# Attention on one core: rings of three PSUM banks for score tiles and row halves, and five instead of six key steps summed on GpSimd

## The chip, the cores and the metric

One core of a Trainium2 chip runs the kernel. The metric is the device time of one execution in microseconds, the median of several.

## The reference, cut to what matters

The input is 8 samples of 256 channels on 32 x 32 positions. Four residual blocks follow one another: a state-space block, an attention block, a block of dilated convolutions, and a second attention block with layer norms around it. All of it is fp32. Both attentions have 8 heads of width 32 over 1024 positions:

```python
x = x + _L0_conv_ref(_gn(x), ...)
x = x + _L1_conv_ref(_gn(x), ...)      # attention
x = x + _L2_conv_ref(_gn(x), ...)
x = x + _L3_conv_ref(_gn(x), ...)      # layer norm, attention, layer norm
# within an attention
scores = jnp.einsum('bthe,bThe->bhtT', q, k) / jnp.sqrt(jnp.float32(EMB))
attn = jax.nn.softmax(scores, axis=-1)
out = jnp.einsum('bhtT,bThe->bthe', attn, v)
```

## The kernel before

The samples run one after the other, and each has two attentions, so there are 16 in all. The five engines have each a program of their own, written out by hand, and wait for each other by counters (`Signal`). The order of each engine's work is the order of its loops.

An attention has four phases (`PHASES`): two groups of four heads (`GH`), times two halves of 512 queries (`NC`). The softmax needs the largest score of each query first, and for that the scores are computed twice:

- **Row halves.** `row_scores(n, cc)` (L1239) computes a 128 x 512 piece of the scores with queries on the partitions, and VectorE reduces it to a maximum per query (`row_max`, L954). A phase needs 32 of them. Those of phase 0 run ahead of the phases. Those of phase ph + 1 are laid between the work of phase ph, `HALF_ROWS` = 5, 4, 4, 4, 5, 5, 5, 0 for its key steps 0 to 7. The last phase has none to do.
- **The turn.** When the 32 are done, VectorE joins them (`mboth`), TensorE transposes them (`turn_max`), ScalarE and VectorE make the negated maxima (`nm`) and SyncE copies these into `QS` by DMA, where they take part in the next phase's score matmuls.
- **Tiles.** A phase has 8 key steps (`KT`). For each, TensorE computes four score tiles of 128 keys x 512 queries, one per head (L1340), and ScalarE takes the exponential from PSUM to the buffer `PT` (L624), which has room for three key steps.
- **Values.** `values(i - 1)` (L1281) multiplies the weights of the key step before with V, four matmuls in four column groups (L1292, eight passes in the trace), which add up in bank 0.
- **Denominators.** The weights must be summed over the keys. Most key steps of a phase are added up element by element on GpSimd (L408, `POOL_SUMS`), in the last phase on VectorE (L1006, `DVE_SUMS`), into `acc`, and one group of matmuls sums `acc` over the partitions into bank 1 (L1311). The key steps that are in no such list are summed on TensorE directly, by four more matmuls with ones (L1301) behind their values.

PSUM has eight banks. In the phases bank 0 holds the output, bank 1 the denominators, banks 2 to 5 the four tiles of a key step, and banks 6 and 7 the two halves of one row. An exponential covers two tiles (1024 columns), and a pair of tiles waits until the exponential of the same pair of the key step before is done. A row half waits for the maximum of the row before (L1249). TensorE's order in key step kt is: tile, tile, row half, tile, tile, row half, values of step kt - 1, then what is left of the row halves, one of them between the values and the direct sum where there is one.

Of the kernel before, what the change touches and what calls it, by code (L numbers as in the profile page):

```python
# [23 lines left out]
P = 128  # L24
# [4 lines left out]
NC = L // N  # L29
HEADS, DH = 8, 32  # L30
GH = 4
GROUPS = HEADS // GH
KT = L // P
# [19 lines left out]
TURN_AT = 7  # L53
AHEAD = 3
NORM_AT = 4
PHASE_ROWS = sum(HALF_ROWS) // NC

POOL_SUMS = (0, 1, 2, 3, 5, 6)
DVE_SUMS = (0, 1, 2, 3, 4, 5, 6)
SMALL_U = 1.0 / 128  # L60

# [31 lines left out]
def build(nc, x, wpack, vpack, w8, out):  # L93
    with ExitStack() as ctx:
        sb = lambda name, shape, dt=F32: ctx.enter_context(nc.sbuf_tensor(name, shape, dt))

        def sig(name, per):
            return Signal(ctx.enter_context(nc.semaphore(name)), per)
# [145 lines left out]
        nm_in = sig("nm_in", 2 * PHASES * 2 * 16)  # L244
        sum_pool = sig("sum_pool", 2 * (PHASES - 1) * (len(POOL_SUMS) - 1))
        sum_dve = sig("sum_dve", 2 * (len(DVE_SUMS) - 1))
        s_ps, p_sb = sig("s_ps", 128), sig("p_sb", 128)
        pv_ps, den_ln, den_rc = sig("pv_ps", 64), sig("den_ln", 8), sig("den_rc", 8)
        o_raw, o_sb = sig("o_raw", 8), sig("o_sb", 8)

# [80 lines left out]
        def _(pool):  # L331
# [35 lines left out]
            def sample(b):  # L367
# [27 lines left out]
                for a in range(2):  # L395
                    for j in range(GH):
                        pool.wait_ge(*stackedq[1][j](b, (a + 1) * 48))
                        pool.wait_ge(*stackedk[1][j](b, (a + 1) * 48))
                    for ph in range(PHASES - 1):
                        if ph == 2:  # L400
                            pool.wait_ge(*pv_ps(b, (PHASES * a + 1) * KT))
                        for k in range(1, len(POOL_SUMS)):
                            i, total = key_step(a, ph, POOL_SUMS[k]), acc[:, ph % 2, :, :]
                            first = PT[:, key_step(a, ph, 0) % 3, :, :] if k == 1 else total
                            if k > 1:
                                pool.wait_ge(*sum_pool(b, pool_sums(a, ph, k - 1)))
                            pool.wait_ge(*p_sb(b, 2 * i + 2))
                            pool.tensor_tensor(total, first, PT[:, i % 3, :, :], ALU.add).then_inc(sum_pool.sem, 1)  # L408
                pool.wait_ge(*x_new(b, 16))

# [5 lines left out]
        def _(act):  # L416
# [160 lines left out]
            def attention(b, a):  # L577
# [34 lines left out]
                for ph in range(PHASES):  # L612
                    for kt in range(KT):
                        i = key_step(a, ph, kt)
                        if kt == 0 and ph >= 1:
                            reciprocals(PHASES * a + ph - 1)
                        if i % (PHASES * KT) >= 3:
                            act.wait_ge(*pv_ps(b, i - 2))
                            done = summed(a, *divmod(i % (PHASES * KT) - 3, KT))
                            if done:  # L620
                                act.wait_ge(*(sum_pool, sum_dve)[done[0]](b, done[1]))
                        for pr in range(2):
                            act.wait_ge(*s_ps(b, 2 * i + pr + 1))
                            act.activation(PT[:, i % 3, 2 * pr:2 * pr + 2, :], PS[:, 2 + 2 * pr:4 + 2 * pr, :],  # L624
                                           ACT.Exp, scale=SCALE).then_inc(p_sb.sem, 1)
                        if kt == TURN_AT and ph < PHASES - 1:
                            neg_max(ph + 1)
# [41 lines left out]
        def _(dve):  # L669
# [269 lines left out]
            def attention(b, a):  # L939
# [60 lines left out]
                for k in range(1, len(DVE_SUMS)):  # L1000
                    i, total = key_step(a, ph, DVE_SUMS[k]), acc[:, ph % 2, :, :]
                    first = PT[:, key_step(a, ph, 0) % 3, :, :] if k == 1 else total
                    if k > 1:
                        dve.wait_ge(*sum_dve(b, dve_sums(a, k - 1)))
                    dve.wait_ge(*p_sb(b, 2 * i + 2))
                    dve.tensor_tensor(total, first, PT[:, i % 3, :, :], ALU.add).then_inc(sum_dve.sem, 1)  # L1006
                normalize(ph)

# [54 lines left out]
        def _(pe):  # L1063
# [161 lines left out]
            def attention(b, a, X):  # L1225
# [13 lines left out]
                def row_scores(n, cc):  # L1239
# [4 lines left out]
                    if c == 0 and q == 0 and cc == 0:  # L1244
                        pe.wait_ge(*stackedq[g][j](b, (a + 1) * 48))
                        pe.wait_ge(*stackedk[g][j](b, (a + 1) * 48))
                    ahead = 2 if ph == 0 else 1
                    if n % PHASE_ROWS >= ahead:
                        pe.wait_ge(*r_max(b, halves(a, n - ahead, cc) + 1))  # L1249
                    pe.matmul(PS[:, row_slot(n, cc), :], QS[0:kd, c, h, q * P:q * P + P], KS[0:kd, h, cc * N:cc * N + N],  # L1250
                              start=True, stop=True).then_inc(r_ps.sem, 1)

# [28 lines left out]
                def values(i, between, turn=None):  # L1281
# [2 lines left out]
                    g = ph // NC  # L1284
                    sums = POOL_SUMS if ph < PHASES - 1 else DVE_SUMS
                    direct = [k for k in range(KT) if k not in sums]
                    pe.wait_ge(*p_sb(b, 2 * i + 2))
                    if kt == 0 and ph > 0:
                        pe.wait_ge(*o_raw(b, i // KT))
                    for j in range(GH):  # L1290
# [24 lines left out]
                for ph in range(PHASES):  # L1315
# [10 lines left out]
                    for kt in range(KT):  # L1326
                        i = key_step(a, ph, kt)
                        row[1] = HALF_ROWS[kt]
                        if kt == 0:
# [2 lines left out]
                            else:  # L1332
                                next_rows(NC)
                            pe.wait_ge(*nm_in(b, 32 * (PHASES * a + ph + 1)))
                        for pr in range(2):
                            if ph + kt > 0:
                                pe.wait_ge(*p_sb(b, 2 * i - 2 + pr + 1))
                            for jj in range(2):
                                h = GH * g + 2 * pr + jj
                                ins = pe.matmul(PS[:, 2 + 2 * pr + jj, :], KS[:, h, kt * P:kt * P + P], QS[:, c, h, :],  # L1340
                                                start=True, stop=True)
                            ins.then_inc(s_ps.sem, 1)
                            next_rows(1)
                        if kt > 0:
                            values(i - 1, next_rows, ph + 1 if kt == TURN_AT and ph < PHASES - 1 else None)
                        next_rows(row[1])
                values(key_step(a, PHASES - 1, KT - 1), lambda most: None)

# [57 lines left out]

def row_slot(n, cc):

    return (4 + 2 * (n % 2) if n < PHASE_ROWS else 6) + cc


def halves(a, n, cc):
# [112 lines left out]
```

## Time and profile before

| | |
|---|---|
| median of 3 runs | 5492.75 us (5491.58 to 5498.53) |
| the profiled execution | 5495.14 us, its span 5493.3 us |
| granted TensorE clock over the span | 0.853 of full speed |
| TensorE matmul busy | 4249.1 us (77%) |
| VectorE busy | 3607.0 us (66%) |
| ScalarE busy | 2146.6 us (39%) |
| GpSimd busy | 2007.6 us (37%) |
| chain that ended last, by engine | TensorE 47%, VectorE 28%, issue 10%, ScalarE 7% |

Busy time says how long an engine was at work, and not whether somebody waited for it. The chain is followed back from the last instruction to what released it, and its shares say on whose work the end depended. In the timeline equal neighbouring instructions are drawn together (x8 is eight of them), the brackets give how long the engine was idle before them and whose work came last, and PEld is the load of the weights for a matmul.

### The profile page before, as it was taken

The numbers are of one execution on the slowest core, as the hardware profiler recorded it, in microseconds if no ns is written. First come the engines' busy times: TensorE is split into PE (matmuls) and PEld (weight loads), VectorE is DVE, ScalarE is ACT, GpSimd is POOL, SyncE is SP. The second block draws the span as 40 slices with busy tenths as digits, with TensorE's granted clock in tenths as the row PEclk, the third lists the DMA queues.
The fourth block names the chain that finished last, engine by engine and source line by source line (L and its number), as shares of the span: only waits on it lengthen the run. The fifth ranks groups of instructions, "written<-read, shape, count | busy, mean of one in ns | idle before, by whom it ended". The sixth has DMA issues, their size and how long they took to land.

```text
span 5493.3 us, 44457 instructions
## 1 busy us (share of the span) xinstructions
PE 4249.1 (77%) x16298; PEld 1843.1 (34%) x16298; DVE 3607.0 (66%) x4793; ACT 2146.6 (39%) x2639; POOL 2007.6 (37%) x681
## 2 busy tenths in 40 slices
PE   5688866879668896688866878669796697866978
PEld 2243422434224332243322433224332243322333
DVE  6763677637776368764687646867468674686746
ACT  3233452334423354243542425424254242542524
POOL 3531435404344043440444504434044340443404
PEclk7689977999769997799977999779897798977999
DMA  0020100210002100022000120011200112001020
GB/s 36 0 55 19 29 8 7 48 29 19 8 8 47 34 14 8 9 47 44 3 8 14 41 46 1 8 25 30 46 1 8 31 24 46 1 8 29 19 46 9
DMA packets 62956, 125.75 MB, mean 23 GB/s; under 512 B 18825, under 2 KB 21001, under 8 KB 62482
## 3 DMA queue, kind: packets, MB, share of 16 engines
q1 hardware_dynamic: 62738, 122.91, 9.6%
q8 instruction: 129, 2.11, 0.2%
q14 instruction: 89, 0.73, 0.0%
HBM read 12.23 MB, written 8.39 MB: 4 GB/s over the span
## 4 chain that ended last, share of the span: by engine, by line
PE 47%; DVE 28%; issue 10%; ACT 7%; SPq 4%; POOL 2%; DMA 2%; DVEq 0%; ACTq 0%; POOLq 0%
DVE mx L954 9%; PE PS L1250 8%; PE PS L1292 8%; PE PS L1087 7%; PE PS L1340 7%; PE PS L1374 4%; DVE work L846 3%; DVE work L848 3%; PE PS L1146 3%; PE PS L1184 2%; ACT PT L624 2%; SPq L290 2%; PE PS L1301 2%; SPq L299 2%; POOL work L392 1%
## 5 line engine op out<-in xcount | busy, mean ns | idle before, releaser
L954 DVE TENSOR_REDUCE mx<-PS 128x1 f32<-128x512 f32 x2048 | 1338.1, 687 | 422.0 <-PE PS L1250 417.9
L624 ACT ACTIVATE PT<-PS 128x1024 f32<-128x1024 f32 x1024 | 1006.9, 1023 | 689.9 <-PE PS L1340 660.0
L1250 PE MATMUL PS<-KS,QS 96*128 96x512 f32 x2048 | 894.9, 479 | 195.4 <-DMA KS<-piece 84.7
L408 POOL TENSOR_TENSOR piece<-PT 128x2048 f32<-128x2048 f32 x48 | 220.0, 4584 | 2183.4 <-ACT PT L624 2183.4
L408 POOL TENSOR_TENSOR piece<-piece,PT 128x2048 f32<-128x2048 f32 x192 | 878.0, 4573 | 58.4 <-ACT PT L624 47.1
L388 POOL TENSOR_TENSOR work<-work,Crep 128x1024 f32<-128x1024 f32 x256 | 616.3, 2409 | 390.5 <-DVE work L846 193.1
L1340 PE MATMUL PS<-QS,KS 98*128 98x512 f32 x2048 | 681.4, 424 | 45.9 <-DMA QS<-nm 22.2
L1250 PEld LDWEIGHTS PS<-KS,QS 96*128 96x128 f32 x2048 | 378.0, 197 | 816.2 <-DVE mx L954 578.0
L1292 PE MATMUL PS<-PT,Vt 128*32 128x512 f32 x4096 | 546.0, 605 | 27.0 <-ACT PT L624 27.0
L1184 PE MATMUL PS<-dstk,sel 128*128 128x512 f32 (+1 forms) x640 | 315.7, 568 | 321.1 <-DVE work L848 133.0
L542 ACT ACTIVATE PS<-PS,Aneg 128x1024 f32<-128x1024 f32 x256 | 278.3, 1087 | 628.5 <-PE PS L1184 597.8
L1184 PE MATMUL PS<-ustk,sel 128*128 128x512 f32 (+1 forms) x640 | 335.3, 597 | 182.9 <-DVE work L831 85.6
L1340 PEld LDWEIGHTS PS<-QS,KS 98*128 98x128 f32 x2048 | 376.5, 197 | 291.0 <-ACT PT L624 164.5
L1087 PE MATMUL PS<-xg,W 128*128 128x512 f32 x640 | 354.0, 709 | 81.1 <-ACT Brep L470 36.3
L1184 PEld LDWEIGHTS PS<-dstk,sel 128*128 128x128 f32 x640 | 152.9, 268 | 460.5 <-DVE work L846 178.9
L1184 PEld LDWEIGHTS PS<-ustk,sel 128*128 128x128 f32 x640 | 139.7, 257 | 491.1 <-DVE work L831 170.5
L1146 PE MATMUL PS<-work,ysel 128*32 128x512 f32 (+1 forms) x1536 | 273.1, 802 | 39.3 <-POOL work L392 30.6
L831 DVE TENSOR_TENSOR work<-PS,Brep 128x1024 f32<-128x1024 f32 (+1 forms) x256 | 250.7, 979 | 71.7 <-PE PS L1184 68.8
L946 DVE SCALAR_TENSOR_TENSOR piece<-PS,V,piece 128x1024 fp32r<-128x1024 f32 x64 | 82.2, 1284 | 278.1 <-ACT piece L588 278.1
L392 POOL TENSOR_TENSOR work<-work,Crep 128x640 f32<-128x640 f32 x128 | 210.5, 1648 | 138.7 <-DVE work L857 80.4
L373 POOL TENSOR_TENSOR ustk<-work,ustk 64x1024 fp32r<-64x1024 f32 x16 | 37.6, 2352 | 587.9 <-ACT ustk L485 587.3
L1087 PEld LDWEIGHTS PS<-xg,W 128*128 128x128 f32 x640 | 144.7, 231 | 263.2 <-issue 182.6
(198 smaller groups left out, 4983.0 us busy)
## 6 DMA issues: line engine op xcount, KB each, us to landing
QS<-piece SPq DMA_DIRECT2D x384, 128.0 KB, 2.4
KS<-piece SPq DMA_DIRECT2D x384, 128.0 KB, 2.4
xin<-x SPq DMA_DIRECT2D x8, 1024.0 KB
out<-xr SPq DMA_DIRECT2D x8, 1024.0 KB, 4.0
W<-wpack SPq DMA_DIRECT2D x2, 1024.0 KB
QS<-nm SPq DMA_DIRECT2D x128, 8.0 KB, 1.9
W<-wpack SPq DMA_DIRECT2D x1, 576.0 KB
W<-wpack SPq DMA_DIRECT2D x2, 256.0 KB
```

Of the source, the lines that this page charges most:

```text
L388: pool.tensor_tensor(slot, h, Crep[:, at:at + L], ALU.mult).then_inc(hC_sb.sem, 1)
L392: pool.tensor_tensor(two(slot), two(h), Crep[:, None, at:at + W3].broadcast_to((P, 2, W3)), ALU.mult).then_inc(hC_sb.sem, 1)
L408: pool.tensor_tensor(total, first, PT[:, i % 3, :, :], ALU.add).then_inc(sum_pool.sem, 1)
L542: act.activation(dst, src, ACT.Exp, scale=Aneg[:, ps * SG + g:ps * SG + g + 1]).then_inc(dA_sb.sem, 1)
L624: act.activation(PT[:, i % 3, 2 * pr:2 * pr + 2, :], PS[:, 2 + 2 * pr:4 + 2 * pr, :], ACT.Exp, scale=SCALE).then_inc(p_sb.sem, 1)
L954: dve.tensor_reduce(mx[:, at, cc:cc + 1], PS[:, row_slot(n, cc), :], AX.X, ALU.max).then_inc(r_max.sem, 1)
L1087: ins = pe.matmul(PS[:, bank, :], w[:, k, m * P:m * P + P], X[:, k, c * N:c * N + N], start=(k == 0), stop=(k == CT - 1))
L1146: ins = pe.matmul(PS[32 * j:32 * j + 32, c, 0:N if ps < 2 else W3], ysel[:, q % 4, :], src, start=(q % 4 == 0), stop=(q % 4 == 3), skip_gr ...
L1184: ins = pe.matmul(PS[:, slot + c, 0:wc], sel[:, g % 8, :], stk[:, g // 8, at + c * N:at + c * N + wc], start=True, stop=True)
L1250: pe.matmul(PS[:, row_slot(n, cc), :], QS[0:kd, c, h, q * P:q * P + P], KS[0:kd, h, cc * N:cc * N + N], start=True, stop=True).then_inc(r_ ...
L1292: ins = pe.matmul(PS[32 * j:32 * j + 32, 0, :], Vt[:, kt, DH * h:DH * h + DH], PT[:, i % 3, j, :], start=(kt == 0), stop=(kt == KT - 1), s ...
L1340: ins = pe.matmul(PS[:, 2 + 2 * pr + jj, :], KS[:, h, kt * P:kt * P + P], QS[:, c, h, :], start=True, stop=True)
```

## The change

- Constants: a ring size of three, and `POOL_SUMS` is (0, 1, 3, 4, 6) instead of (0, 1, 2, 3, 5, 6). Key steps 2, 5 and 7 of phases 0 to 2 are then summed directly on TensorE, where it was 4 and 7.
- Tiles take banks 2, 3 and 4 in turn, each tile by itself: it waits for the exponential three tiles back, and has a signal of its own. The exponential covers one tile (512 columns), four per key step where there were two.
- Row halves of phases 1 to 3 take banks 5, 6 and 7 in turn and wait for the maximum three halves back. Phase 0 stays at banks 4 to 7 and the wait of four halves.
- TensorE's order in key step kt is: tile, row half, tile, row half, values of step kt - 1 (with a row half ahead of the direct sum, where there is one), tile, row half, tile, row half.
- Who waits for the weights of a key step counts four signals instead of two.

```diff
--- before.py
+++ after.py
@@ -53,9 +53,10 @@
 TURN_AT = 7
 AHEAD = 3
 NORM_AT = 4
+RING = 3
 PHASE_ROWS = sum(HALF_ROWS) // NC
 
-POOL_SUMS = (0, 1, 2, 3, 5, 6)
+POOL_SUMS = (0, 1, 3, 4, 6)
 DVE_SUMS = (0, 1, 2, 3, 4, 5, 6)
 SMALL_U = 1.0 / 128
 
@@ -244,7 +245,7 @@
         nm_in = sig("nm_in", 2 * PHASES * 2 * 16)
         sum_pool = sig("sum_pool", 2 * (PHASES - 1) * (len(POOL_SUMS) - 1))
         sum_dve = sig("sum_dve", 2 * (len(DVE_SUMS) - 1))
-        s_ps, p_sb = sig("s_ps", 128), sig("p_sb", 128)
+        s_ps, p_sb = sig("s_ps", 256), sig("p_sb", 256)
         pv_ps, den_ln, den_rc = sig("pv_ps", 64), sig("den_ln", 8), sig("den_rc", 8)
         o_raw, o_sb = sig("o_raw", 8), sig("o_sb", 8)
 
@@ -404,7 +405,7 @@
                             first = PT[:, key_step(a, ph, 0) % 3, :, :] if k == 1 else total
                             if k > 1:
                                 pool.wait_ge(*sum_pool(b, pool_sums(a, ph, k - 1)))
-                            pool.wait_ge(*p_sb(b, 2 * i + 2))
+                            pool.wait_ge(*p_sb(b, GH * i + GH))
                             pool.tensor_tensor(total, first, PT[:, i % 3, :, :], ALU.add).then_inc(sum_pool.sem, 1)
                 pool.wait_ge(*x_new(b, 16))
 
@@ -619,9 +620,9 @@
                             done = summed(a, *divmod(i % (PHASES * KT) - 3, KT))
                             if done:
                                 act.wait_ge(*(sum_pool, sum_dve)[done[0]](b, done[1]))
-                        for pr in range(2):
-                            act.wait_ge(*s_ps(b, 2 * i + pr + 1))
-                            act.activation(PT[:, i % 3, 2 * pr:2 * pr + 2, :], PS[:, 2 + 2 * pr:4 + 2 * pr, :],
+                        for j in range(GH):
+                            act.wait_ge(*s_ps(b, GH * i + j + 1))
+                            act.activation(PT[:, i % 3, j, :], PS[:, score_slot(i % (PHASES * KT), j), :],
                                            ACT.Exp, scale=SCALE).then_inc(p_sb.sem, 1)
                         if kt == TURN_AT and ph < PHASES - 1:
                             neg_max(ph + 1)
@@ -1002,7 +1003,7 @@
                     first = PT[:, key_step(a, ph, 0) % 3, :, :] if k == 1 else total
                     if k > 1:
                         dve.wait_ge(*sum_dve(b, dve_sums(a, k - 1)))
-                    dve.wait_ge(*p_sb(b, 2 * i + 2))
+                    dve.wait_ge(*p_sb(b, GH * i + GH))
                     dve.tensor_tensor(total, first, PT[:, i % 3, :, :], ALU.add).then_inc(sum_dve.sem, 1)
                 normalize(ph)
 
@@ -1244,9 +1245,9 @@
                     if c == 0 and q == 0 and cc == 0:
                         pe.wait_ge(*stackedq[g][j](b, (a + 1) * 48))
                         pe.wait_ge(*stackedk[g][j](b, (a + 1) * 48))
-                    ahead = 2 if ph == 0 else 1
-                    if n % PHASE_ROWS >= ahead:
-                        pe.wait_ge(*r_max(b, halves(a, n - ahead, cc) + 1))
+                    ahead = 2 * NC if ph == 0 else RING
+                    if NC * (n % PHASE_ROWS) + cc >= ahead:
+                        pe.wait_ge(*r_max(b, halves(a, n, cc) - ahead + 1))
                     pe.matmul(PS[:, row_slot(n, cc), :], QS[0:kd, c, h, q * P:q * P + P], KS[0:kd, h, cc * N:cc * N + N],
                               start=True, stop=True).then_inc(r_ps.sem, 1)
 
@@ -1284,7 +1285,7 @@
                     g = ph // NC
                     sums = POOL_SUMS if ph < PHASES - 1 else DVE_SUMS
                     direct = [k for k in range(KT) if k not in sums]
-                    pe.wait_ge(*p_sb(b, 2 * i + 2))
+                    pe.wait_ge(*p_sb(b, GH * i + GH))
                     if kt == 0 and ph > 0:
                         pe.wait_ge(*o_raw(b, i // KT))
                     for j in range(GH):
@@ -1332,17 +1333,14 @@
                             else:
                                 next_rows(NC)
                             pe.wait_ge(*nm_in(b, 32 * (PHASES * a + ph + 1)))
-                        for pr in range(2):
-                            if ph + kt > 0:
-                                pe.wait_ge(*p_sb(b, 2 * i - 2 + pr + 1))
-                            for jj in range(2):
-                                h = GH * g + 2 * pr + jj
-                                ins = pe.matmul(PS[:, 2 + 2 * pr + jj, :], KS[:, h, kt * P:kt * P + P], QS[:, c, h, :],
-                                                start=True, stop=True)
-                            ins.then_inc(s_ps.sem, 1)
+                        for j in range(GH):
+                            if GH * (KT * ph + kt) + j >= RING:
+                                pe.wait_ge(*p_sb(b, GH * i + j - RING + 1))
+                            pe.matmul(PS[:, score_slot(i % (PHASES * KT), j), :], KS[:, GH * g + j, kt * P:kt * P + P],
+                                      QS[:, c, GH * g + j, :], start=True, stop=True).then_inc(s_ps.sem, 1)
                             next_rows(1)
-                        if kt > 0:
-                            values(i - 1, next_rows, ph + 1 if kt == TURN_AT and ph < PHASES - 1 else None)
+                            if j == 1 and kt > 0:
+                                values(i - 1, lambda most: next_rows(1) if most == 1 else None, ph + 1 if kt == TURN_AT and ph < PHASES - 1 else None)
                         next_rows(row[1])
                 values(key_step(a, PHASES - 1, KT - 1), lambda most: None)
 
@@ -1406,7 +1404,12 @@
 
 def row_slot(n, cc):
 
-    return (4 + 2 * (n % 2) if n < PHASE_ROWS else 6) + cc
+    return 4 + 2 * (n % 2) + cc if n < PHASE_ROWS else 5 + (NC * (n % PHASE_ROWS) + cc) % RING
+
+
+def score_slot(i, j):
+
+    return 2 + (GH * i + j) % RING
 
 
 def halves(a, n, cc):
```

## Rows read from the trace of the kernel before

**Rows 1.** Costliest groups (page, section 5): busy us, mean ns, idle before, releaser

```profile
L954 DVE TENSOR_REDUCE mx<-PS 128x1 f32<-128x512 f32 x2048 | 1338.1, 687 | 422.0 <-PE PS L1250 417.9
L624 ACT ACTIVATE PT<-PS 128x1024 f32<-128x1024 f32 x1024 | 1006.9, 1023 | 689.9 <-PE PS L1340 660.0
...
L408 POOL TENSOR_TENSOR piece<-piece,PT 128x2048 f32<-128x2048 f32 x192 | 878.0, 4573 | 58.4 <-ACT PT L624 47.1
```

**Rows 2.** Busy time by stretch: phases 0, 1 and 3 of the first attention

```profile
328.28:361.29 33.01, 29.55 (x133) 14.29 (x137) 21.81 (x34) 16.14 (x17) 22.60 (x5) 0.88 0.01 1
361.29:394.27 32.98, 30.77 (x157) 12.70 (x159) 22.92 (x36) 17.01 (x19) 22.91 (x6) 1.00 0.01 2
...
427.24:454.16 26.92, 22.61 (x136) 7.25 (x135) 16.39 (x11) 17.85 (x20) 0.25 (x1) 1.00 0.01 1
```

**Rows 3.** Timeline, an ordinary key step: start us, length us, engine line operation [idle before]

```profile
340.09 1.06 PE L1292 MATMUL PS<-PT,Vt 128*32 128x512 f32 x8
341.08 0.30 PEld L1250 LDWEIGHTS PS<-KS,QS 96*128 96x128 f32 x2 [0.84 <-DVE mx L954]
...
341.62 2.68 DVE L954 TENSOR_REDUCE mx<-PS 128x1 f32<-128x512 f32 x4 [0.73 <-PE PS L1250]
341.65 0.62 PE L1340 MATMUL PS<-QS,KS 98*128 98x512 f32 x2
342.36 0.19 PEld L1250 LDWEIGHTS PS<-KS,QS 96*128 96x128 f32 x1 [0.52 <-DVE mx L954]
...
342.70 0.63 PE L1340 MATMUL PS<-QS,KS 98*128 98x512 f32 x2
...
343.17 0.40 PE L1250 MATMUL PS<-KS,QS 96*128 96x512 f32 x1
...
343.50 1.06 PE L1292 MATMUL PS<-PT,Vt 128*32 128x512 f32 x8
```

**Rows 4.** Timeline, a key step whose weights TensorE sums directly

```profile
351.00 1.07 PE L1292 MATMUL PS<-PT,Vt 128*32 128x512 f32 x8
...
352.42 1.07 PE L1301 MATMUL PS<-PT,ones 128*32 128x512 f32 x8
...
353.42 0.30 PEld L1250 LDWEIGHTS PS<-KS,QS 96*128 96x128 f32 x2 [0.84 <-DVE mx L954]
```

**Rows 5.** Timeline, from one phase to the next

```profile
359.19 1.94 ACT L624 ACTIVATE PT<-PS 128x1024 f32<-128x1024 f32 x2 [2.45 <-PE PS L1340]
...
359.48 1.06 PE L1292 MATMUL PS<-PT,Vt 128*32 128x512 f32 x8
...
361.18 1.07 PE L1292 MATMUL PS<-PT,Vt 128*32 128x512 f32 x8 [0.43 <-ACT PT L624]
...
364.03 1.06 PE L1311 MATMUL PS<-piece,ones 128*32 128x512 f32 x8
...
366.33 3.85 ACT L624 ACTIVATE PT<-PS 128x1024 f32<-128x1024 f32 x4
...
369.62 1.07 PE L1292 MATMUL PS<-PT,Vt 128*32 128x512 f32 x8
```

**Rows 6.** Timeline, the last phase

```profile
427.12 1.07 PE L1292 MATMUL PS<-PT,Vt 128*32 128x512 f32 x8 [0.42 <-ACT PT L624]
...
430.00 0.77 PEld L1340 LDWEIGHTS PS<-QS,KS 98*128 98x128 f32 x4 [1.01 <-DMA QS<-nm]
...
433.78 1.07 PE L1292 MATMUL PS<-PT,Vt 128*32 128x512 f32 x8
...
438.26 1.06 PE L1292 MATMUL PS<-PT,Vt 128*32 128x512 f32 x8
...
440.11 1.94 ACT L624 ACTIVATE PT<-PS 128x1024 f32<-128x1024 f32 x2 [0.42 <-PE PS L1340]
...
448.75 1.07 PE L1292 MATMUL PS<-PT,Vt 128*32 128x512 f32 x8 [0.42 <-ACT PT L624]
```

**Rows 7.** Groups by line and shape, ScalarE on one bank

```profile
L605 ACT ACTIVATE lr<-PS 128x512 f32<-128x512 f32 x64 | 38.2, 597 | 215.3 <-PE PS L1311 215.3
```

## The prediction

> **What bounds the kernel now.** I read three views: the costliest groups, then the busy time of each engine phase by phase, then the timeline of single key steps. In the groups [rows 1] the reader is to see that VectorE's row maxima and ScalarE's exponentials spend a third to two thirds of a busy time waiting for TensorE, so neither sets the pace, and that one GpSimd sum takes 4.57 us. By stretch [rows 2] a phase with row halves lasts 33.0 us, of which TensorE is busy 30.8, VectorE 22.9, GpSimd 22.9 and ScalarE 17.0. The last phase has no row halves and lasts 26.9 us. TensorE is thus the nearest bound, and the question is what its order waits for.
>
> I call V(k) the values group of key step k (eight passes), T0 to T3 the four score tiles of a step, R a row half, D the four direct sums of the weights. In an ordinary step [rows 3] one V starts at 340.09 and the next at 343.50, so 3.41 us. Inside it: V holds TensorE for 0.99 us before the next weight load, and its next matmul starts about 1.10 us after V did. Two matmuls take 0.47 us (342.70 to 343.17), so 0.235 each; a matmul ahead of a V takes 0.33. One R waits for VectorE's maximum (load at 342.36, where without the wait it would be at 342.0). With four R, four T and a V and no wait the step is 7 x 0.235 + 0.33 + 1.10 = 3.08 us. So 0.33 us of a step is the row wait that a deeper ring of banks can take away.
>
> **Part 1, three banks for row halves.** From phase 1 on an R waits for the maximum three halves back instead of two (one row). An R's result reaches VectorE 0.43 us after the matmul starts (load 341.08, matmul about 341.19, maximum at 341.62), four maxima take 2.68, so 0.67 each, and a freed bank is written again about 0.17 us after its maximum ends [rows 3]. In the new order T0 R T1 R V T2 R T3 R the halves come at 0.24, 0.71, 2.37 and 2.84 of a 3.08 us step, and 4 x 0.67 = 2.68 us of maxima fit in it, so the wait goes: steps 1 and 2 cost 3.08 each instead of 3.41. Steps with five halves need 3.35 us of maxima, and there VectorE is what is late next: followed half by half, V(3) to V(4) and V(4) to V(5) come out at 3.63 us each.
>
> **Part 2, GpSimd sums five steps instead of six.** It removes one sum of 4.57 us [rows 1] per phase 0 to 2 and adds a D on TensorE. V to D with one R between is 1.42 us, and the next load is 1.00 us after D starts [rows 4]. So a D costs 1.42 - 0.33 = 1.09 us beyond what the step has anyway, up to 1.42 if the R finds no other place. It is wanted at step 2 because the first sum starts only when step 1's weights are complete and frees the buffer of step 0 4.6 us later. Steps of 3.08 would make step 3's exponentials wait about 2 us for that; with D(2) ahead of T2 in that step, they have caught up. I get 4.35 us for V(2) to V(3) (before: 3.41). The D that was at step 4 moves to step 5. V(5) to V(6), with D, five halves and the wait of T1 for the exponential of T2, is 4.2 us. The later sums lie in the open, with GpSimd at 4 x 4.57 = 18.3 us of a 32 us phase.
>
> **Part 3, three banks for tiles, one tile per exponential, V after T1.** ScalarE on one bank: a 512-wide instruction takes 597 ns [rows 7], and 1023 ns for 1024 columns less 0.427 for half of them agrees. Four in a row of 1024 take 3.85 us [rows 5], so (3.85 - 1.02)/3 = 0.94 from start to start, and 0.94 - 0.43 = 0.51 for 512. A step's four cost about 2.05 us instead of 1.9, which nobody waits for where a step is 3.1 us. What matters is the order. V(k) waits for all four exponentials of step k. Before, all four tiles of step k+1 stand between V(k-1) and V(k), and those of step k ran a whole V earlier. Now T2 and T3 of step k stand behind V(k-1), and only T0 and T1 of the next step are between them and V(k). This closes a chain from each V to the next: V to T2 1.10, T2 to its exponential 0.51 (a V at 438.26 and the exponential of the second tile behind it at 440.11 [rows 6] are 1.85 apart, less 1.10 and 0.235), T2's exponential 0.51 until T3's can start, T3's 0.60, and 0.05 to V. The sum is 2.77 us.
>
> With row halves TensorE's own 3.08 us is longer and the chain is hidden. In **the last phase** nothing else fills the time. Before, V(0) at 433.78 and V(7) at 448.75 [rows 6] are 14.97 us apart, 2.14 a step. Now 7 x 2.77 = 19.4, so +4.4 us. The phase's start gains a little, since V(0) no longer follows four tiles of step 1: exponentials of step 0 start 4.02 after the V(7) before it, T3 needs the first one and its exponential ends at 6.15, so V(0) comes 6.2 after that V(7), against 6.66 (427.12 to 433.78 [rows 6]); the wait for the row of maxima (430.00) stays. The last phase: -0.5 + 4.4 = +3.9 us. VectorE's sums there (2.3 us each) keep up with 2.77.
>
> **Turns between phases** lose for the same reason. Before, V(6) at 359.48 and V(7) at 361.18 [rows 5] are 1.70 apart, as all tiles of step 7 stood ahead of V(6). Now T2 and T3 come after V(6) and the transpose: T2 at 1.35, T3 at 1.6, exponentials 1.86 to 2.97, V(7) at 3.0. The exponentials of the new phase start 5.15 us after V(7) as before (361.18 to 366.33, behind the two reciprocal steps), T3 waits for the first, and V(0) comes at 7.5 instead of 8.44 (361.18 to 369.62). GpSimd's last sum starts when step 6 is complete, about at V(6), and ends 4.7 us later; the matmuls on it come at 3.0 + 2.85, so it stays hidden (before the last phase they come at 3.0 + 1.74 and the cover is nearly gone).
>
> **Sum of phase 1 and 2**, V(7) to V(7): 7.5 + 3.08 + 3.08 + 4.35 + 3.63 + 3.63 + 4.2 + 3.0 = 32.45 against 32.98 [rows 2], -0.5 us each. Phase 0 has 0.45 more from V(0) to V(7) by the same terms (24.95 against 32.98 - 8.44 = 24.54), and gains between nothing and 0.9 at its start, where the clock is low for a while (0.88 over the phase [rows 2]); I take zero, with ends -0.5 and +0.5. An attention: 0 - 0.5 - 0.5 + 3.9 = +2.9 us; sixteen (eight samples, two each): +46 us. Against the profiled execution: its span of 5493.3 lies in a time of 5495.14, which is 2.4 above the median. 5495.1 + 46 = 5541 for such an execution, 5539 for the median.
>
> Ends of the terms: if the time from V to the second exponential is 0.1 us off either way, 7 x 16 x 0.1 = 11 us; the turns and five-half steps are worked out and not seen, 0.6 us per phase either way is 48 x 0.6 = 29 us. The forecast's own range is 5500 to 5580.
>
> **Rivals.** Faster: the split pays everywhere. ScalarE is idle a third of the last phase [rows 2], smaller pieces free banks sooner, and if TensorE stayed at 2.14 us a step there, only the gains are left: 16 x (-1.0 - 0.5) = -24, so 5469 us. It decides where V to V in the last phase is under 2.35 us. For it: TensorE's own work for V and four tiles is about 2.1 us. Against it: each term of the chain has a row. The Trainium skill says this too (Perfetto Trace Analysis, Optimizing Scalar/DVE Operations: breaking up instructions may allow work to be completed sooner where Scalar isn't saturated but causes bubbles elsewhere). By that rule the time would be the 5469 of this rival; no row here has the tiles split.
>
> The row ring brings nothing: VectorE or ScalarE stays late in phases 0 to 2 and only the loss is left, 16 x 3.9 = 62, so 5555 us, and up to 5590 if the first sum also stalls a phase. For it: 22.9 us of VectorE in a phase, in bursts.
>
> The clock falls in the last phase. TensorE would be at work some 2.1 of 2.77 us, while it was busy 22.6 of 26.9 us at full clock before [rows 2]. At 1.2 GHz the matmul parts of the chain (1.10, 0.235, 0.4) about double, up to +1.5 us a step, 7 x 16 x 1.5 = 168, so about 5700. Against it: the gaps stay near 0.6 us, and phase 1 holds 1.00 over gaps of that size at its turn [rows 2, 5]. The Trainium skill (TensorE: Matmul & The Clock Gate, A second HAM failure mode: psum-queue depth-cycling) names a kernel whose clock swung because TensorE idled briefly between groups as it went round its banks; by that rule this rival would be the time.
>
> **Chances.** The forecast 0.60; ring brings nothing 0.14; clock 0.04; faster 0.12; gains and losses about equal 0.10. A measurement here can tell about 0.2%, 11 us, from no change. Faster 0.12, same 0.10, slower 0.78. The range 5490 to 5590 holds the forecast's range and most of the second rival.
>
> **What would show it.** Right: in the last phase V to V at 2.7 to 2.8 us, each V released by ScalarE, and TensorE's share down; in phases 1 and 2 steps 1 and 2 at 3.1 us with no wait for maxima; V(6) to V(7) at 3.0; GpSimd four sums a phase with no exponential waiting for it. Wrong: V to V under 2.35 in the last phase; phases 1 and 2 away from 32.5 us by over 0.6; step 3's exponentials held by GpSimd; a granted clock under 1.00 in the last phase.

## The result, and the profile after

The changed kernel took 5509.25 us (median of 7, 5501.85 to 5514.26) against 5491.58 us before (median of 7, 5489.31 to 5498.53). The ratio is 1.0028, with a 95% interval of 1.0018 to 1.0037: 0.3% slower. The profiled execution took 5512.06 us with a span of 5510.3. I had forecast 5539 and a range of 5490 to 5590. The time lies in that range, but the loss is 18 us where 46 were forecast.

The page of the changed kernel: first the busy time of each engine, then the groups that answer to [rows 1] (busy us, mean ns of one, idle before it and its releaser). Code lines up to 1312 are one further down than before, and the tile matmul is L1339 here (in runs x2, x3, x7 and x8 L1340).

```profile
PE 4282.5 (78%) x16682; PEld 1865.3 (34%) x16682; DVE 3558.2 (65%) x4793; ACT 2223.1 (40%) x3663; POOL 1786.1 (32%) x633
...
L955 DVE TENSOR_REDUCE mx<-PS 128x1 f32<-128x512 f32 x2048 | 1289.9, 683 | 402.8 <-PE PS L1251 401.3
L625 ACT ACTIVATE PT<-PS 128x512 f32<-128x512 f32 x2048 | 1083.7, 599 | 627.0 <-PE PS L1339 541.0
...
L409 POOL TENSOR_TENSOR piece<-piece,PT 128x2048 f32<-128x2048 f32 x144 | 658.3, 4571 | 250.0 <-ACT PT L625 246.2
```

The reader is to see that no engine became the bound: the row maxima wait 402.8 us for TensorE, as before (422.0), and a single-bank exponential takes 599 ns.

Phases 0, 1 and 3 of the first attention, to be held against [rows 2]. The columns are length, then busy us of TensorE's matmuls, its weight loads, VectorE, ScalarE and GpSimd, the granted clock and DMA.

```profile
326.11:357.76 31.65, 29.11 (x141) 14.24 (x145) 20.89 (x34) 17.38 (x33) 16.46 (x4) 0.90 0.01 1
357.76:389.46 31.70, 30.49 (x165) 12.99 (x167) 21.80 (x36) 18.22 (x35) 18.29 (x5) 1.00 0.01 2
421.13:451.55 30.42, 24.46 (x136) 7.63 (x136) 16.39 (x11) 18.87 (x36) 1.85 (x1) 1.00 0.01 1
```

Phases 0 and 1 are shorter than before (33.01 and 32.98), the last one is longer (30.42 against 26.92; both of these stretches run on some 2.5 us past the end that the table below takes). To put all 16 attentions on one footing I took the start of ScalarE's copy of the maxima at each turn, and for the end of the last phase the start of its reciprocal (`lr`), 64 of each in a trace. Sums over the 16 attentions, in us:

| | phase 0 | phase 1 | phase 2 | last phase | all the rest of the span |
|---|---|---|---|---|---|
| before | 529.8 | 527.5 | 527.4 | 394.3 | 3514.4 |
| after | 525.3 | 507.1 | 507.1 | 458.7 | 3512.2 |
| difference | -4.5 | -20.4 | -20.3 | +64.4 | -2.2 |

So the result is a small difference of two larger things: the phases with row halves gain 45 us, and the last phases lose 64. A phase 1 or 2 takes 31.69 us (32.96 before). A last phase takes 28.14 in ten of 16 attentions (24.63 before). In five others, 29.3 to 31.4 long, its mean granted clock is 0.94 or 0.84 instead of 1.00, which adds 8 us; one takes 28.5.

The distances between the starts of the values groups, V(7) of the phase before first, tell where within a phase (phase 1 and last phase of the first attention; the terms of the forecast add up to 32.47, where the prediction wrote 32.45):

| | V7-V0 | V0-V1 | V1-V2 | V2-V3 | V3-V4 | V4-V5 | V5-V6 | V6-V7 | sum |
|---|---|---|---|---|---|---|---|---|---|
| phase 1 before | 8.44 | 3.41 | 3.41 | 3.41 | 4.13 | 4.84 | 3.64 | 1.70 | 32.98 |
| phase 1 forecast | 7.5 | 3.08 | 3.08 | 4.35 | 3.63 | 3.63 | 4.2 | 3.0 | 32.47 |
| phase 1 after | 7.42 | 3.08 | 3.06 | 4.28 | 3.54 | 3.54 | 4.10 | 2.68 | 31.70 |
| last before | 6.66 | 2.12 | 2.36 | 2.15 | 2.35 | 2.16 | 2.35 | 1.48 | 21.63 |
| last after | 6.41 | 2.67 | 2.67 | 2.68 | 2.67 | 2.68 | 2.66 | 2.68 | 25.12 |

The timeline of the changed kernel in the last phase (start, length, engine, line, operation, idle before and releaser), against [rows 6]:

```profile
432.77 1.06 PE L1293 MATMUL PS<-PT,Vt 128*32 128x512 f32 x8
...
433.77 0.53 PEld L1339 LDWEIGHTS PS<-QS,KS 98*128 98x128 f32 x3 [0.84 <-ACT PT L625]
...
434.31 2.07 ACT L625 ACTIVATE PT<-PS 128x512 f32<-128x512 f32 x4 [0.61 <-PE PS L1339]
434.96 0.19 PEld L1339 LDWEIGHTS PS<-QS,KS 98*128 98x128 f32 x1 [0.66 <-ACT PT L625]
...
435.45 0.16 PEld L1293 LDWEIGHTS PS<-PT,Vt 128*32 128x32 f32 x8 [0.30 <-ACT PT L625]
```

This is the chain of the prediction, link by link. V starts at 432.77, the tiles behind it at 433.77, ScalarE is free and waits for them until 434.31 (0.61 idle). The first two of its four exponentials are of these tiles: the second starts 0.49 us after the first and ends about 435.40, and the next V starts at 435.45. The load at 434.96 is a tile of the next step, which waits for the first of them. The 0.84 in brackets at 433.77 is no such wait: it stands at the first load behind every V, while TensorE is at work on V. In [rows 6] the exponentials came in pairs and TensorE had four tiles to do between two V.

### The profile page after: what moved, and what is told of

Read it like the earlier page. It is cut to its first block, busy times and chain, and to the rows that moved or that the text cites. A ratio compares the mean times of both kernels' runs of the same rounds, so it can differ in the third digit from the quotient of the medians.

```text
span 5510.3 us, 46153 instructions
## 1 busy us (share of the span) xinstructions
PE 4282.5 (78%) x16682; PEld 1865.3 (34%) x16682; DVE 3558.2 (65%) x4793; ACT 2223.1 (40%) x3663; POOL 1786.1 (32%) x633
## 3 DMA queue, kind: packets, MB, share of 16 engines
q8 instruction: 132, 2.16, 0.2%
## 4 chain that ended last, share of the span: by engine, by line
PE 51%; DVE 22%; issue 10%; ACT 7%; SPq 4%; POOL 3%; DMA 2%; DVEq 0%; ACTq 0%; POOLq 0%
PE PS L1339 10%; PE PS L1293 9%; PE PS L1251 7%; PE PS L1088 6%; DVE mx L955 4%; PE PS L1372 4%; DVE work L847 3%; DVE work L849 3%; ACT PT L625 3%; PE PS L1302 3%; PE PS L1147 3%; PE PS L1185 2%; SPq L291 2%; SPq L300 2%; POOL work L393 1%
## 5 line engine op out<-in xcount | busy, mean ns | idle before, releaser
L955 DVE TENSOR_REDUCE mx<-PS 128x1 f32<-128x512 f32 x2048 | 1289.9, 683 | 402.8 <-PE PS L1251 401.3
L625 ACT ACTIVATE PT<-PS 128x512 f32<-128x512 f32 x2048 | 1083.7, 599 | 627.0 <-PE PS L1339 541.0
L1339 PE MATMUL PS<-QS,KS 98*128 98x512 f32 x2048 | 850.4, 448 | 65.4 <-ACT PT L625 42.0
L409 POOL TENSOR_TENSOR piece<-piece,PT 128x2048 f32<-128x2048 f32 x144 | 658.3, 4571 | 250.0 <-ACT PT L625 246.2
L1339 PEld LDWEIGHTS PS<-QS,KS 98*128 98x128 f32 x2048 | 390.0, 197 | 615.5 <-ACT PT L625 439.7
L1251 PEld LDWEIGHTS PS<-KS,QS 96*128 96x128 f32 x2048 | 406.8, 200 | 449.8 <-DVE mx L955 217.0
L1040 DVE TENSOR_TENSOR xr<-xr,rl 128x512 f32<-128x512 f32 x32 | 22.2, 692 | 325.8 <-ACT rl L648 325.8
```

Source lines behind the costliest of these rows:

```text
L625: act.activation(PT[:, i % 3, j, :], PS[:, score_slot(i % (PHASES * KT), j), :], ACT.Exp, scale=SCALE).then_inc(p_sb.sem, 1)
L955: dve.tensor_reduce(mx[:, at, cc:cc + 1], PS[:, row_slot(n, cc), :], AX.X, ALU.max).then_inc(r_max.sem, 1)
L1339: pe.matmul(PS[:, score_slot(i % (PHASES * KT), j), :], KS[:, GH * g + j, kt * P:kt * P + P], QS[:, c, GH * g + j, :], start=True, stop=Tr ...
```

## Experiments

Each was compared with runs of the kernel before on the same chip, whose median was 5498.4 us beside x1 to x4 and 5495.3 us beside x5 to x8. Steps and phases are read from one profiled execution of each. x4 is an edit of the kernel before, all others are edits of the changed kernel. The question of x1 to x3 is the last phase: is it the order of the values, the number of banks, or the width of the exponentials?

**x1, order alone.**

```diff
-                            if j == 1 and kt > 0:
+                            if j == (3 if ph == PHASES - 1 else 1) and kt > 0:
```

> The changed kernel, with one edit in the last phase: the values of the key step before come after the fourth tile instead of after the second; the ring stays at three banks. Theory (a chain of values, tiles 2 and 3, their exponentials, next values costs 2.67 us a step against 2.14 before the change): that chain is broken, but with three banks the fourth tile of a step must wait for the exponential of the first tile of the same step, and values follow it. From the rows of the changed kernel: values to exponential 1.53, exponential 0.60, to the matmul 0.16, to the values 0.33 = 2.6 to 2.7 us. So V to V stays about 2.65, the phase about 28 us and the time 5500 to 5512. Rival (the order alone is the cause): 2.1 to 2.2 a step, the last phase 24.6 us, the time 5510 - 16 x 3.5 = about 5453.

Measured: 5519.2 us, ratio 1.0036 (1.0023 to 1.0050). V to V in the last phase is 2.67 to 2.69. At full clock the phase is 27.5 us; in 11 of 16 attentions the clock fell in it. The steps came out as expected; the time is 7 us above the range, and the profiled execution, the shortest of five (5510.0), does not show what the others spent more.

```profile
435.19 1.06 PE L1293 MATMUL PS<-PT,Vt 128*32 128x512 f32 x8
436.19 0.53 PEld L1339 LDWEIGHTS PS<-QS,KS 98*128 98x128 f32 x3 [0.84 <-ACT PT L625]
...
436.80 2.06 ACT L625 ACTIVATE PT<-PS 128x512 f32<-128x512 f32 x4 [0.62 <-PE PS L1339]
437.45 0.19 PEld L1339 LDWEIGHTS PS<-QS,KS 98*128 98x128 f32 x1 [0.74 <-ACT PT L625]
...
437.88 0.16 PEld L1293 LDWEIGHTS PS<-PT,Vt 128*32 128x32 f32 x8 [0.24 <-ACT PT L625]
```

The fourth tile's load (437.45) waits 0.74 us for the exponential of the first tile of the same step, which began at 436.80, and the values follow it. The chain of the change is gone and another of the same length has its place, as expected. The order alone is not enough.

**x3, six banks alone.** In the last phase the row halves need no bank, so the tiles can go round banks 2 to 7.

```diff
     def score_slot(i, j):
-        return 2 + (GH * i + j) % RING
+        m, last = GH * i + j, GH * KT * (PHASES - 1)
+        return 2 + m % RING if m < last else 2 + (m - last) % (2 * RING)
...
-                            if GH * (KT * ph + kt) + j >= RING:
-                                pe.wait_ge(*p_sb(b, GH * i + j - RING + 1))
+                            deep = 2 * RING if ph == PHASES - 1 else RING
+                            if GH * (KT * ph + kt) + j >= deep:
+                                pe.wait_ge(*p_sb(b, GH * i + j - deep + 1))
```

> The changed kernel with only the six banks for tiles in the last phase, values after the second tile as in the change. Theory (the chain goes from values through tiles 2 and 3 of the order to the next values, and no bank is in it): 2.67 us a step as in the changed kernel, 5500 to 5512. Rival (three banks are too few for tiles): the step falls to 2.2 and the time to about 5455.

Measured: 5509.2 us, ratio 1.0021 (1.0012 to 1.0030), V to V 2.67 us in the steps at full clock. The clock fell in 13 of the 16 last phases, where it was five after the change, and the profiled execution (5517.3) is the longest of ten. At full clock the phase takes 28.14 us, the same as after the change: twice the banks change nothing in its length while V stands after the second tile.

**x2, both.**

> Both edits in the last phase: values after the fourth tile, and tiles go round six banks (2 to 7), since the row halves need none there. Theory: neither chain is left, so a step costs what TensorE's own work costs (values 1.1, four tiles 0.94, 0.1) or four exponentials of 0.5, 2.1 to 2.2 us; the last phase 24.0 to 24.8 us instead of 28.1 to 31.4, and the swings of the clock in it go with the gaps: 5510 - 16 x 3.5 - 8 = 5440 to 5455. Rival (the single-bank exponentials themselves make the last phase slow, four a step instead of two): a step stays over 2.5 us and the time over 5490.

Measured: 5430.5 us, ratio 0.9877 (0.9862 to 0.9892), better than both kernels and a little better than expected. V to V is 2.13 us, the last phases are 23.9 us in 14 of 16 attentions, 383.2 in sum (458.7 after the change), and their clock is 1.00 in all 16. The rest of the span outside the phases is 9 us shorter too, where nothing was edited; that part is not explained.

```profile
433.89 0.16 PEld L1293 LDWEIGHTS PS<-PT,Vt 128*32 128x32 f32 x8 [0.36 <-ACT PT L625]
433.89 1.07 PE L1293 MATMUL PS<-PT,Vt 128*32 128x512 f32 x8
434.88 0.77 PEld L1340 LDWEIGHTS PS<-QS,KS 98*128 98x128 f32 x4 [0.84 <-ACT PT L625]
434.88 1.21 PE L1340 MATMUL PS<-QS,KS 98*128 98x512 f32 x4
436.02 0.16 PEld L1293 LDWEIGHTS PS<-PT,Vt 128*32 128x32 f32 x8 [0.37 <-ACT PT L625]
```

Four loads in a row (434.88, x4), 0.99 us behind the start of V as everywhere, with no wait between them, and the next V 2.13 us after the last. So the loss of the last phase is made by the two together, the place of V and the three banks: undoing the banks alone brings back nothing, and undoing the order alone 0.6 us of 4.2. The single-bank exponentials are not to blame: with them the phase is 0.7 us shorter than it was before the change (24.63). No run tells whether four or five banks would do.

**x7, the turn.** x2, and in step 7 of phases 0 to 2 V also stands after the fourth tile.

```diff
-                            if j == (3 if ph == PHASES - 1 else 1) and kt > 0:
+                            if j == (3 if ph == PHASES - 1 or kt == TURN_AT else 1) and kt > 0:
```

> x2 with a further edit: in step 7 of phases 0 to 2 the values also come after the fourth tile (three banks there). Theory: V(6) comes 0.5 to 0.7 us later, since the fourth tile waits for the first exponential, but the four exponentials are then nearly done and V(7) follows after 1.2 to 1.4 us instead of 2.68: V(5) to V(7) 6.3 instead of 6.78, so -0.5 us in 48 phases, -24 against x2. Rival (the turn of the maxima sets the pace there): no gain against x2.

Measured: 5402.5 us, ratio 0.9828 (0.9813 to 0.9843), 28 us under x2 (25 us when each is held against its own runs of the kernel before; 24 were expected). Phases 1 and 2 take 31.18 us instead of 31.69. Of the 95 us between the spans of this run and the kernel before, 17 lie outside the phases and are not explained.

```profile
387.38 0.19 PEld L1340 LDWEIGHTS PS<-QS,KS 98*128 98x128 f32 x1 [0.36 <-ACT PT L625]
...
387.82 1.06 PE L1293 MATMUL PS<-PT,Vt 128*32 128x512 f32 x8
388.81 0.09 PEld L1256 LDWEIGHTS PS<-ident,mboth 128*16 128x16 f32 x1 [0.84 <-issue]
...
389.02 0.16 PEld L1293 LDWEIGHTS PS<-PT,Vt 128*32 128x32 f32 x8
389.02 1.07 PE L1293 MATMUL PS<-PT,Vt 128*32 128x512 f32 x8
```

The fourth tile does wait (387.38), but V(7) starts at 389.02, 1.20 us after V(6) at 387.82. V(5) to V(7) is 5.07 + 1.20 = 6.27 us, where it was 4.09 + 2.68 = 6.77. So the chain through V, two tiles and their exponentials also cost time at the turns. Ahead of the last phase half a microsecond of it is lost again: V(7) to V(0) is 6.91 there and was 6.41, as the matmuls on GpSimd's sum now wait 0.59 us for it.

**x6, part 1 undone.** Everything kept but the third bank for row halves.

```diff
-    return ... else 5 + (NC * (n % PHASE_ROWS) + cc) % RING
+    return ... else 5 + (NC * (n % PHASE_ROWS) + cc) % 2
...
-                    ahead = 2 * NC if ph == 0 else RING
+                    ahead = 2 * NC if ph == 0 else 2
```

> The changed kernel with the row halves on two banks, waiting two halves back: part 1 undone, all the rest kept. Theory (the third bank is what takes the wait for maxima away): in the new order the first half of a step comes 0.93 us after the third of the step before and needs its maximum, 0.42 + 0.69 + 0.17 later than its matmul, so some 0.25 to 0.35 us a step, seven steps, 48 phases: +80 to +120, 5590 to 5630. Rival (laying halves singly between tiles is enough): under 5530.

Measured: 5631.3 us, ratio 1.0250 (1.0234 to 1.0265), a little above the range. A phase 1 or 2 takes 34.78 us instead of 31.69, an ordinary step 3.54 instead of 3.08, so 0.46 more and not 0.25 to 0.35.

```profile
371.78 0.19 PEld L1251 LDWEIGHTS PS<-KS,QS 96*128 96x128 f32 x1 [0.51 <-DVE mx L955]
...
372.38 0.19 PEld L1251 LDWEIGHTS PS<-KS,QS 96*128 96x128 f32 x1 [0.30 <-DVE mx L955]
```

Both late row halves of a step wait for a maximum again (0.51 and 0.30 us idle). The third bank is worth 3.1 us a phase. It is the part that earns: without it these phases are longer than in the kernel before (34.78 against 32.96, with one direct sum more), although the halves are laid singly. No run lays them singly in the old order.

**x4, part 2 alone,** in the kernel before.

```diff
-POOL_SUMS = (0, 1, 2, 3, 5, 6)
+POOL_SUMS = (0, 1, 3, 4, 6)
```

> The kernel before with only the new list of GpSimd's key steps (0, 1, 3, 4, 6): part 2 alone. Theory: one more direct sum on TensorE costs 1.09 to 1.42 us in each of 48 phases and nobody waited for the sum it removes, so +52 to +68, 5544 to 5560. Rival (GpSimd's chain of five sums held something up before): less than half of that, under 5518.

Measured: 5544.1 us, ratio 1.0082 (1.0065 to 1.0099), so the total falls on the lower end of what was expected, by luck, for the way there is another one. A phase 1 or 2 takes 33.50 us, only 0.53 more than before and not 1.09 to 1.42: V(2) to V(3) grows by 0.85, V(4) to V(5) shrinks by 0.74, V(5) to V(6) grows by 0.37, as the two direct sums take over time in which row halves waited before. Between V(0) and V(6) of phase 1 the loads that wait for a maximum have 3.0 us of idle time ahead of them where they had 4.0 (the 0.84 behind every V left out), and none of these waits stands in a step with a direct sum. The last phases, in which nothing was edited, take 422.7 us instead of 394.3. There the mean granted clock is 0.88 to 0.94 in 15 of 16 attentions (1.00 in all of the kernel before); the one last phase at 1.00 takes 24.64 us, as before. Stretches of the first one (columns as above, the third from the right is the clock):

```profile
431.60:433.60 2.00, 1.20 (x4) 0.67 (x4) 0.68 (x1) 1.94 (x3) 0.00 (x0) 1.00 0.00 0
433.60:435.60 2.00, 1.56 (x4) 0.76 (x4) 0.51 (x2) 2.00 (x3) 0.00 (x0) 0.81 0.00 0
435.60:437.60 2.00, 2.00 (x9) 0.20 (x8) 0.48 (x1) 1.15 (x2) 0.00 (x0) 0.50 0.00 0
437.60:439.60 2.00, 2.00 (x16) 1.03 (x12) 1.81 (x1) 0.80 (x1) 0.00 (x0) 0.83 0.00 0
```

**x5, part 2 undone,** in the changed kernel.

```diff
-POOL_SUMS = (0, 1, 3, 4, 6)
+POOL_SUMS = (0, 1, 2, 3, 5, 6)
```

> The changed kernel with GpSimd's old list of key steps (0, 1, 2, 3, 5, 6): part 2 undone. The changed trace shows the exponentials of step 3 held by GpSimd's first sum until 1.21 us after the values of step 2, covered by the direct sum there. Theory: without that direct sum the hold is open for a moment, V(2) to V(3) is about 3.4 instead of 4.28, and the direct sum that moves from step 5 to step 4 costs the same there: -0.9 us in 48 phases, -42, so about 5467. Rival (the reason to drop a sum is sound, the faster steps make everyone wait for GpSimd): 5505 or more.

Measured: 5507.5 us (5492.0 to 5516.0), ratio 1.0019 (1.0008 to 1.0030), so no difference to the changed kernel (1.0018 to 1.0037) can be told. My theory failed here. The step it spoke of came out (V(2) to V(3) 3.51 instead of 4.28), but GpSimd's last sum now ends too late at the turn:

```profile
422.62 1.04 PE L1302 MATMUL PS<-PT,ones 128*32 128x512 f32 x8
...
425.06 1.06 PE L1312 MATMUL PS<-piece,ones 128*32 128x512 f32 x8 [1.39 <-POOL piece L409]
```

The group of matmuls on the sum waits 1.39 us for GpSimd ahead of the last phase, and V(7) to V(0) is 7.90 instead of 7.42 at the other turns. Only phase 0, which has no such turn ahead of it, gains what was expected (1.0 us on average). Phases 1 and 2 gain 0.50 and 0.43 us, and the last phase gives back 1.3 us or more (29.4 in most attentions, 28.14 after).

**x8, all and six sums:** x7 with the old list.

> x7 with GpSimd's old list of six key steps. If x5's theory holds: a further -40 against x7, about 5380 to 5400, better than both kernels. If GpSimd is the bound of the faster phases (five sums of 4.57 us and a first one that starts late make 27 us of a phase of 31): no gain or a loss against x7.

Measured: 5417.4 us, ratio 0.9855 (0.9839 to 0.9872), 15 us over x7, so here too the rival holds. Phases 1 and 2 stay at 31.2 us, phase 0 gains 0.5 on average, the last phase is 25.5 or more instead of 24.1, and in six of 16 its clock falls. Dropping the sum is right once the rest is fast: with six sums GpSimd's chain is the last to arrive at every turn, and ahead of the last phase TensorE waits 1.95 us for it.

```profile
426.36 1.07 PE L1312 MATMUL PS<-piece,ones 128*32 128x512 f32 x8 [1.95 <-POOL piece L409]
```

The best version of the study is x7, 1.7% under the kernel before and about 2% under the changed one.

## Why the prediction was right and wrong

**Direction and mechanism** were right, by a small margin: without the clock, of which more below, the loss is 9 us and not 17. The chain of the last phase was forecast at 2.77 us a step and is 2.67; x1 to x3 confirm the theory that its links are V, the tiles behind it and their exponentials. The last phase was forecast at +3.9 us and costs +3.51 at full clock, and +4.0 on average. So the agreement of +64 us with +62 is luck in part: the steps cost 56 us, and the other 8 are time at the lower clock, which the forecast did not have in it. Two misses stand in the 3.51: seven steps cost 3.74 and not 4.4, and the start gains 0.25 and not 0.5. There GpSimd's last sum is already the last to arrive, which I had called "nearly" covered:

```profile
418.43 4.55 POOL L409 TENSOR_TENSOR piece<-piece,PT 128x2048 f32<-128x2048 f32 x1 [2.11 <-ACT PT L625]
...
423.04 0.16 PEld L1312 LDWEIGHTS PS<-piece,ones 128*32 128x32 f32 x8 [1.00 <-POOL piece L409]
```

 The sum ends at 422.98, and the matmuls on it start 0.06 us later and 1.14 behind the direct sum, where that distance is 0.86 before the change. The exponentials of the phase then start 4.31 us after V(7) and not 4.02.

**The step that failed is the sum of phases 1 and 2**: 32.45 forecast, 31.70 measured, so -1.27 us a phase and not -0.5. Over 32 such phases that is about 25 of the 29 us between the forecast (46) and the two spans (17). The prediction's own sign of being wrong, these phases away from 32.5 us by over 0.6, came true. The mechanism held, and the sizes of terms were off. By the table above the 0.77 us are 0.32 at V(6) to V(7), 0.18 in the two five-half steps, 0.10 at V(5) to V(6), 0.08 at V(7) to V(0), 0.07 at V(2) to V(3) and 0.02 in the ordinary steps:

- V(6) to V(7), "T2 at 1.35": forecast 3.0, measured 2.68, which is 0.32 of the 0.77. I had let the first matmul start 1.10 us after V and the transpose hold up the tiles behind it by 0.25. In the changed kernel they start at 1.03:

```profile
388.21 1.09 ACT L625 ACTIVATE PT<-PS 128x512 f32<-128x512 f32 x2 [0.56 <-PE PS L1339]
```
```profile
386.67 1.07 PE L1293 MATMUL PS<-PT,Vt 128*32 128x512 f32 x8
387.67 0.28 PE L1256 MATMUL PS<-ident,mboth 128*16 128x128 f32 x1
387.70 0.70 PE L1339 MATMUL PS<-QS,KS 98*128 98x512 f32 x2
```

 The transpose starts 1.00 us after V and the tiles 0.03 us behind it, and the exponential starts 1.54 us after V, not 1.86.
- V to the exponential of the first tile behind it, in every chain: I took 1.10 + 0.51 = 1.61, from a row for the second tile less one matmul. Measured 434.31 - 432.77 = 1.54. The first matmul behind a V starts with its load, 1.00 us after V (432.77 to 433.77, and 340.09 to 341.08 in [rows 3]), and not at 1.10; its result reaches the next engine 0.54 later. This makes the chain of the last phase 0.07 shorter. It is also part of V(2) to V(3) and V(5) to V(6), where no run takes the rest of the miss apart.
- The pace of the row maxima, "0.67 each": I divided the length of four by four (2.68 / 4, [rows 3]). The first start to the last end holds one full latency of 0.69, and in that row VectorE could also start the third and fourth only 0.67 and 0.70 us after the one before. In the changed kernel four take 2.48 and five 3.08 us:

```profile
369.92 2.48 DVE L955 TENSOR_REDUCE mx<-PS 128x1 f32<-128x512 f32 x4 [0.60 <-PE PS L1251]
...
377.27 3.08 DVE L955 TENSOR_REDUCE mx<-PS 128x1 f32<-128x512 f32 x5 [0.88 <-PE PS L1251]
...
378.01 0.19 PEld L1251 LDWEIGHTS PS<-KS,QS 96*128 96x128 f32 x1 [0.29 <-DVE mx L955]
...
378.61 0.19 PEld L1251 LDWEIGHTS PS<-KS,QS 96*128 96x128 f32 x1 [0.30 <-DVE mx L955]
```

 From start to start that is 0.60. So the steps with five halves, which I took as bound by VectorE at 3.63, are 3.54 with two idle times of 0.3 us ahead of late halves.

**Part 1 as a whole** went the way forecast: 3.08 and 3.06 in the ordinary steps (3.08 forecast), and x6 shows that the third bank is the cause.

**Part 2** was half right. In the changed kernel the step with the new direct sum costs what I worked out (4.28 against 4.35), and GpSimd's hold on step 3's exponentials is hidden by it as forecast:

```profile
371.21 1.07 PE L1293 MATMUL PS<-PT,Vt 128*32 128x512 f32 x8
...
372.42 1.08 ACT L625 ACTIVATE PT<-PS 128x512 f32<-128x512 f32 x2 [1.65 <-POOL piece L409]
...
372.64 1.06 PE L1302 MATMUL PS<-PT,ones 128*32 128x512 f32 x8
```

 But I counted the sum's removal as worth nothing beyond that hold. x5 and x8 show that dropping it also keeps the turns free: with the sixth sum the matmuls on the sum wait 1.39 us ahead of the last phase, which makes the exchange even.

**Phase 0** was put at zero and gained 0.28 us on average, within its ends. From V(0) to V(7) I had it 0.45 longer (the two numbers given for it are 0.41 apart); it is as long as before (24.5, median), by the same terms that were too large in phases 1 and 2. Its lengths spread (31.67 to 34.51) with the clock at its start, and no run takes that apart.

**The clock** was a rival with a chance of 0.04 and a price of 168 us. It came, in small: in five last phases the clock falls to 0.50 for some 3 to 10 us near their start, which costs 8 us in sum. The lines are of x3, the first attention, the clock third from the right, and below them V there:

```profile
428.82:430.82 2.00, 0.83 (x4) 0.35 (x2) 1.18 (x2) 2.00 (x5) 0.00 (x0) 1.00 0.00 0
430.82:432.82 2.00, 1.43 (x8) 0.20 (x8) 0.00 (x0) 1.50 (x4) 0.00 (x0) 0.65 0.00 0
432.82:434.82 2.00, 2.00 (x8) 1.16 (x4) 0.00 (x0) 0.73 (x2) 0.00 (x0) 0.50 0.00 0
434.82:436.82 2.00, 1.93 (x13) 0.66 (x12) 1.54 (x1) 1.40 (x4) 0.00 (x0) 1.00 0.00 0
```
```profile
431.39 1.93 PE L1293 MATMUL PS<-PT,Vt 128*32 128x512 f32 x8 [1.74 <-ACT PT L625]
```

 In the stretch before it fell, TensorE was busy 0.83 of 2 us, and ahead of V at 431.39 it idled 1.74 us for the first exponentials; at the lower level (0.50, so 1.2 of 2.4 GHz) V takes 1.93 us instead of 1.07. What decides whether it falls stays open. It stayed at 1.00 in every last phase of the kernel before, of x2 and of x7; in x4, whose last phase has the order of before, it fell in 15, in x3 in 13, in x1 in 11, in x8 in six, in x5 in five and in x6 in four. Nor do idle times tell the attentions of one kernel apart: in the changed kernel TensorE idles 0.97 us for the exponentials at that place both where the clock then falls and where it stays, and in the kernel before, where it never falls, 0.98. The Trainium skill (TensorE: Matmul & The Clock Gate, A second HAM failure mode: psum-queue depth-cycling) names short idle times between groups as a cause of such swings. By that rule the whole last phase of the changed kernel, where TensorE has about 0.5 us a step without work (2.67 less the 2.13 of x2), should swing, and cost up to 168 us. The trace does not agree: in 11 last phases the clock never leaves 1.00, and in the other five it is back at 1.00 after 3.4 us (10.2 in one) and stays there through the same steps.

**The faster rival** was set beside a rule of the Trainium skill (Perfetto Trace Analysis, Optimizing Scalar/DVE Operations: break up operations that cause bubbles elsewhere). The changed kernel did not gain in its last phase by it. x2 did: V(0) to V(7) is 14.49 us, where it was 14.97 before the change, and V(0) comes 0.26 us earlier. The rule agrees with x2, where TensorE's order has no place that waits for a piece issued just ahead. How much of that is the smaller pieces and how much the six banks no run shows, as none has two-bank exponentials in six banks.

In sum, measured against forecast: phases 1 and 2 -41 against -16, phase 0 -4.5 against 0, last phases +64 against +62, elsewhere -2 against 0; 17 against 46. The rival that gains and losses are about equal (0.10) came nearer than the forecast (0.60). The stretches between attentions shift by -4 to +3 us each, which is not explained.

## What to carry to other kernels

Before shortening a step, write down the closed chains between two engines for the new order, as V, tiles behind V, exponentials, next V; a consumer that is moved up between producers closes one, and where other work used to fill the step it is hidden, and where none does it is the step. A deeper ring and a better order may each be worth little (nothing and 0.6 us of a phase here) and the pair of them 4 us, so try them together. A term that many steps share wants its pace from start to start of a run of instructions (length less one latency, over count less one), and not the length over the count.

## What the runs showed of the hardware

Exponentials of one bank run at 0.49 us from start to start (four in 2.07 us, one 0.60) where two banks take 0.94, so halving them cost ScalarE only 0.02 us per tile. Row maxima of 128 x 512 from PSUM run at 0.60 from start to start with a latency of 0.69. A transpose of 128 columns between a values group and the next matmuls held those up by 0.03 us. And the granted clock can fall in one part of a kernel because of an edit in another: in x4 the edit was in phases 0 to 2, where the clock stayed as it was, and over half of its loss (28.5 of 50 us between the spans) was in the last phases.
